# Causal attention: the mask of the scores by query moves from a TensorE matmul into VectorE's row maximum, and the maxima are split after their transpose

## The reference

```python
h = _layernorm(x, axis=-1) * (1 + ca) + sa
qkv = jnp.einsum('btc,fc->btf', h, W_attn)          # 16 heads of 32 channels
att = jnp.einsum('bhqd,bhkd->bhqk', q, k)
att = jnp.where(causal, att, -jnp.inf)
att = jax.nn.softmax(att / jnp.sqrt(32.), axis=-1)
out = jnp.einsum('bhqk,bhkd->bhqd', att, v)         # then W_proj
x = x + ga * attention
x = x + gb * mlp(modulated layernorm of x)          # three layers: 512-1024-1024-512
```

## Time and profile before

| | |
|---|---|
| median of 3 runs | 1666.01 us (1664.12 to 1668.75) |
| the profiled execution | 1668.86 us |
| its span | 1667.1 us |
| mean granted TensorE clock | 0.972 |
| PE busy | 1536.4 us, 92% of the span |
| DVE busy | 1000.6 us, 60% |
| ACT busy | 644.2 us, 39% |
| POOL busy | 370.6 us, 22% |

### The profile page before, as it was taken

One profiled execution on the slowest core, in us unless ns is written; L12 is line 12 of the kernel. 1 busy time (PEld: TensorE's weight loads), 2 busy tenths in 40 slices (PEclk: granted clock), 3 DMA queues, 4 the chain that ended last, 5 costly groups with the idle time before them and its releaser, 6 DMA issues.

```text
span 1667.1 us, 33396 instructions
## 1 busy us (share of the span) xinstructions
PE 1536.4 (92%) x12032; PEld 1345.7 (81%) x12032; DVE 1000.6 (60%) x2287; ACT 644.2 (39%) x1346; POOL 370.6 (22%) x360
## 2 busy tenths in 40 slices
PE   5499989898989898985699999999999999999998
PEld 1377777787777777874699999999999999999998
DVE  2477878878788878773844444445444454444442
ACT  2146666666666666674512122121212122121211
POOL 0224555454555554553000000000000000000000
PEclk9699999999999999996799999999999999999999
DMA  5162534243425252423600111001100011011100
GB/s 227 43 162 62 127 73 123 71 120 76 121 69 134 58 135 62 110 71 112 204 26 20 45 45 45 13 31 44 44 30 27 31 44 44 0 51 37 44 14 13
DMA packets 75272, 116.98 MB, mean 70 GB/s; under 512 B 10568, under 2 KB 27976, under 8 KB 74704
## 3 DMA queue, kind: packets, MB, share of 16 engines
q1 hardware_dynamic: 68816, 107.31, 23.4%
q10 hardware_dynamic: 6400, 8.92, 1.5%
HBM read 48.52 MB, written 16.81 MB: 39 GB/s over the span
## 4 chain that ended last, share of the span: by engine, by line
PE 51%; DVE 1%; DMA 1%; SPq 0%; ACT 0%; issue 0%; POOL 0%; DVEq 0%; POOLq 0%
PE feature L1203 33%; PE token L1184 16%; PE feature L1174 1%; PE token L1165 1%; DVE w L1115 1%; DMA b_rows<-b 0%; DMA w_ring<-wproj_t 0%; DVE y L1069 0%; SPq L945 0%; DVE y L1067 0%; ACT w L1021 0%; DVE attn_tiles L1093 0%; POOL mlp_rstd L982 0%; DVE gated L1077 0%; DVE res_tiles L1080 0%
## 5 line engine op out<-in xcount | busy, mean ns | idle before, releaser
L454 POOL TENSOR_TENSOR prob_lo<-prob,prob_hi 128x512 f16<-128x512 f32 x256 | 302.0, 1183 | 362.0 <-ACT prob L536 361.0
L1203 PE MATMUL feature<-y,w 128*128 128x256 f32 x3072 | 377.5, 284 | 5.1 <-DVE w L1115 5.1
L1203 PEld LDWEIGHTS feature<-y,w 128*128 128x128 f32 x3072 | 374.2, 190 | 6.7 <-DVE w L1115 5.3
L1015 ACT ACTIVATE mlp_full<-feature,b_cols 128x256 f32<-128x256 f32 x256 | 120.4, 476 | 647.0 <-PE feature L1203 617.4
L1067 DVE CAST y<-mlp_full 128x256 fp32r<-128x256 f32 x256 | 75.2, 294 | 302.4 <-ACT mlp_full L1015 302.1
L529 ACT ACTIVATE prob_hi<-key_score 128x512 f16<-128x512 f32 x320 | 192.3, 601 | 143.0 <-PE key_score L770 140.9
L708 PE MATMUL lin<-h_parts,wqkv 128*128 128x512 f32 x768 | 215.1, 403 | 9.5 <-DVE h_parts L585 9.5
L1203 PEld LDWEIGHTS feature<-turned,w 128*128 128x128 f32 x1536 | 189.2, 191 | 5.1 <-DVE w L1115 3.8
L1203 PE MATMUL feature<-turned,w 128*128 128x256 f32 x1536 | 189.7, 284 | 3.4 <-DVE turned L1069 3.4
L536 ACT ACTIVATE prob<-key_score 128x512 f32<-128x512 f32 x320 | 192.4, 601 | 0.0
L982 POOL TENSOR_TENSOR mlp_rstd<-mlp_var_eps,mlp_minus_half 128x2 f32<-128x2 f32 x16 | 11.1, 696 | 799.3 <-DVE mlp_var_eps L1088 799.3
(11 more groups left out here) (95 smaller groups left out, 1902.8 us busy)
## 6 DMA issues: line engine op xcount, KB each, us to landing
stack<-qk_parts SPq DMA_DIRECT2D x384, 128.0 KB, 2.4
x_tiles<-x SPq DMA_DIRECT2D x32, 256.0 KB, 3.1
attn_dram<-o_rows SPq DMA_DIRECT2D x32, 256.0 KB, 2.2
attn_tiles<-attn_dram SPq DMA_DIRECT2D x16, 512.0 KB, 4.4
res_tiles<-x SPq DMA_DIRECT2D x16, 512.0 KB, 3.6
out<-res_tiles ACTq DMA_DIRECT2D x16, 512.0 KB, 2.8
wmod_sb<-wmod SPq DMA_DIRECT2D x4, 1536.0 KB, 16.4
w_ring<-w_t SPq DMA_DIRECT2D x12, 512.0 KB, 6.2
```

Source lines behind the costliest of these rows:

```text
L454: nc.gpsimd.tensor_tensor(prob_lo[:, key[1] % 2, u, :], prob[:, u, :], prob_hi[:, key[1] % 2, u, :], ALU.subtract).then_inc(lo_pool, 1)
L1015: nc.scalar.activation(full[:, f % 2, :], fbank[f % 4][:, 0:CH], ACT.Relu, bias=bias[:, f:f + 1])\
L1203: mm = nc.tensor.matmul(fbank[f % 4][:, 0:CH], weights[:, wl, c, f * P:(f + 1) * P], data[:, dl, c, :], start=(c == 0 and i == 0), stop=(c ...
```

## The change

TensorE no longer writes the mask of the scores by query: only the mask by key is left (`mask_by_key`), and the first score matmul of a step starts its bank. `row_mask` is a tile of 128 x 512 in bf16, zero but for the triangle in its last 128 columns. VectorE adds its last n columns to a score tile of n columns, writes the sum back into the bank and takes the row maximum of it in the same instruction (`tensor_tensor_reduce`, line 672 of the changed kernel). Step 4, which took both of its tiles in one reduction, now has one instruction for each.

The maxima go on in another way: TensorE transposes the 8 columns of maxima as they are, ScalarE takes minus the transposed rows at step 1 into rows 0 to 7 of `max_rows`, VectorE makes the rest from the same PSUM bank at step 2 into rows 32 to 39, and SyncE, no longer ScalarE, issues the two DMAs, at step 2 of its own list. `max_rows` has one buffer where it had two, so ScalarE first waits until the DMAs of the pair before have landed.

Three more moves: ScalarE writes h twice from PSUM, once as float32 and once rounded, so that VectorE's rounding copy (line 583) goes, and TensorE's bank of a TURN item is free once ScalarE has read it; the lowest part of the values is made on GpSimd (`v_lowest`), no longer on VectorE; and the waits on `v_split` are counted anew (`v_before`).

```diff
-                nc.gpsimd.memset(mask_qk[:], 0.0).then_inc(pool_step, 1)
+                nc.gpsimd.memset(row_mask[:], 0.0).then_inc(pool_step, 1)
...
+                    turned = behind(b, p, 1, first)
+                    if u == 2 and turned:
+                        n, q = turned
+                        wait_apart(sp, turn_taken, 1 + PAIRS * n + q + 1, (o_out[0], 16))
+                        for part in range(2):
+                            sp.dma_start(f32(stack[3 * D + part:3 * D + part + 1, 0, 2 * q:2 * q + 2, :]),
+                                         f32(max_rows[LOW_ROWS * part:LOW_ROWS * part + 2 * NT, :]))\
+                                .then_inc(max_in[q], 16)
...
+                pool.wait_ge(v_mid_ready, v_no(n, g, t) + 1)
+                nc.gpsimd.tensor_tensor(v[:, t, hs, 0:D], rest, v[:, t, hs, 2 * D:3 * D], ALU.subtract)\
+                    .then_inc(v_split, 1)
...
-                nc.scalar.activation(full[:, c % 2, :], lin_bank_of((TURN, c))[:], ACT.Identity,
-                                     scale=mod_now[:, NC_ + c:NC_ + c + 1], bias=mod_now[:, c:c + 1])\
-                    .then_inc(lin_act, 1)
+                if c >= 2:
+                    act.wait_ge(lin_taken, LIN_CREDITS + lin_no(n, (TURN, c - 2)) + 1)
+                for made in (full[:, c % 2, :], h[:, 0, c, :]):
+                    last = nc.scalar.activation(made, lin_bank_of((TURN, c))[:], ACT.Identity,
+                                                scale=mod_now[:, NC_ + c:NC_ + c + 1], bias=mod_now[:, c:c + 1])
+                last.then_inc(lin_act, 1)
...
-                        nc.scalar.copy(max_rows[:, q % 2, :], turn_bank[0:4 * NT, 0:P]).then_inc(turn_taken, 1)
-                        act.wait_ge(turn_taken, 1 + PAIRS * n + q + 1)
-                        for part in range(2):
-                            act.dma_start(
-                                f32(stack[3 * D + part:3 * D + part + 1, 0, 2 * q:2 * q + 2, :]),
-                                f32(max_rows[2 * NT * part:2 * NT * (part + 1), q % 2, :]))\
-                                .then_inc(max_in[q], 16)
+                        act.wait_ge(max_in[(q - 1) % PAIRS], 32 * (n + 1 if q else n))
+                        nc.scalar.activation(max_rows[0:2 * NT, :], turn_bank[0:2 * NT, 0:P], ACT.Copy, scale=-1.0)\
+                            .then_inc(max_hi, 1)
...
-                        if u == 4:
-                            last = nc.vector.reduce_max(row_max[:, p % 2, :, 1],
-                                                        bank[:].rearrange("p (h k) -> p h k", h=2), AX.X)
-                        else:
-                            for _, hh, t, col in (r for r in BY_QUERY if r[0] == u):
-                                last = nc.vector.reduce_max(row_max[:, p % 2, hh, t:t + 1],
-                                                            bank[:, col:col + P * (t + 1)], AX.X)
+                        dve.sem_inc(score_seen, 1)
+                        for _, hh, t, col in (r for r in BY_QUERY if r[0] == u):
+                            n = P * (t + 1)
+                            last = nc.vector.tensor_tensor_reduce(
+                                out=bank[:, col:col + n], in0=bank[:, col:col + n], in1=row_mask[:, T - n:T], scale=1.0,
+                                scalar=LOWEST, op0=ALU.add, op1=ALU.max, accum_out=row_max[:, p % 2, hh, t:t + 1])
...
+                    turned = behind(b, p, 1, first)
+                    if u == 2 and turned:
+
+                        n, q = turned
+                        dve.wait_ge(max_hi, PAIRS * n + q + 1)
                         nc.vector.scalar_tensor_tensor(
-                            out=neg_max[:, p % 2, 1, :].bitcast(F32R), in0=peak, scalar=-1.0,
-                            in1=neg_max[:, p % 2, 0, :], op0=ALU.mult, op1=ALU.subtract).then_inc(max_ready, 1)
+                            out=max_rows[LOW_ROWS:LOW_ROWS + 2 * NT, :], in0=turn_bank[0:2 * NT, 0:P], scalar=-1.0,
+                            in1=f32(max_rows[0:2 * NT, :]), op0=ALU.mult, op1=ALU.subtract).then_inc(turn_taken, 1)
...
-                    nc.tensor.matmul(diagonals(bank, u, False), ident_bf[:], mask_for(mask_qk, u),
-                                     start=True, stop=False, skip_group_check=True)
```

More of the change, by code:

```diff
@@ L42 @@
 MASKED = -1e30
+LOWEST = -3.0e38
+LOW_ROWS = 32
 EPS = 1e-5
@@ L228, with diagonals @@
 LO_ON_DVE = (2,)
-def diagonals(bank, u, by_key):
-    first = {t: col if by_key else col + P * t for u2, _, t, col in (BY_KEY if by_key else BY_QUERY) if u2 == u}
+def diagonals(bank, u):
+    first = {t: col for u2, _, t, col in BY_KEY if u2 == u}
     if u in (0, 2):
@@ L311, in attention @@
     row_max = mem.sb("row_max", [P, 2, 2, NT])
-    neg_max = mem.sb("neg_max", [P, 2, 2, 2 * NT])
-    max_rows = mem.sb("max_rows", [4 * NT, 2, P], F32R)
+    max_rows = mem.sb("max_rows", [LOW_ROWS + 2 * NT, P], F32R)
     prob = mem.sb("prob", [P, UNITS, 512])
@@ L350, in v_no, with v_before @@
         return V_UNITS * n + NT * g + t
+    def v_before(g, t):
+        place = ORDER.index((V, g, t))
+        return max([NT * o[1] + o[2] + 1 for i, o in enumerate(ORDER[:place]) if o[0] == V and (place - i) % 2 == 0],
+                   default=0)
     def unit_no(b, p, u):
@@ L447, in _, with v_lowest @@
             pool.wait_ge(ones_ready, 2)
+            def v_lowest(n, item):
+                if item[0] != V or not last_item(item):
+                    return
+                g, t = item[1:3]
+                hs = slice(g * H // 2, (g + 1) * H // 2)
+                rest = full[:, ORDER.index((V, g, t)) % 2, 0:C // 2].rearrange("p (h d) -> p h d", d=D)
+                pool.wait_ge(v_mid_ready, v_no(n, g, t) + 1)
+                nc.gpsimd.tensor_tensor(v[:, t, hs, 0:D], rest, v[:, t, hs, 2 * D:3 * D], ALU.subtract)\
+                    .then_inc(v_split, 1)
+            for item in before_first():
+                v_lowest(0, item)
             def slot(b, p, first, more):
@@ L468, in slot @@
                             .then_inc(o_scaled, 1)
+                    for n, item in work(b, p, u, more):
+                        v_lowest(n, item)
                     if p == 2 and u == 4 and more:
@@ L619, in after_item @@
                     v_rest(n, item[1], item[2])
-            def step_after_item(n, item):
-                if item[0] == V and last_item(item):
-                    v_lowest(n, item[1], item[2])
             row_stats(0, range(NT))
@@ L722, in do_item @@
                 if item[0] == TURN or item[-1] == 0:
-                    pe.wait_ge(lin_taken, lin_no(n, unit_of(item)) + 1)
+                    place = ORDER.index(unit_of(item))
+                    if ORDER[place - 2][0] == TURN:
+                        pe.wait_ge(lin_act, lin_no(n, unit_of(item)) - 1)
+                    else:
+                        pe.wait_ge(lin_taken, lin_no(n, unit_of(item)) + 1)
                 if item[0] == TURN:
@@ L797, in slot @@
                     key = behind(b, p, 2, first)
-                    masks(b, p, u, key)
+                    if key:
+                        mask_by_key(*key, u)
                     if p < PAIRS:
```

76 lines of the change are left out of this document (28 added, 48 removed).

## The result

The changed kernel takes 1724.42 us (median of 4 runs, 1721.98 to 1728.28), the kernel before, run beside it, 1667.38 (1664.12 to 1670.23): 1.0345 times as long, interval 1.0316 to 1.0374. Forecast were 1716 us and 1684 to 1762.

The account below looks back on a forecast made before the run. PE was taken to bound attention, busy 78.14 of 85 us. From 1668.9 us, +37 for slots, +2 for the last batch and +11 for the clock made 1719; the median lies 2.9 lower, so 1716 us, range 1684 to 1762.

Parts of the forecast that it names:

- The path from step 2 to the landing: From step 2's scores by key to the maxima's DMAs landing: 5.6 us, where PE needs 5.02 in that slot.
- Slot by slot: Attention's slots: slots 0 to 2 and 4 shorter, 3 and 5 to 7 longer; +5.3 us a batch, +37 over seven.
- the half clock that was counted apart: Behind the stall ahead of slot 0: 3.2 us at half speed, 1.6 us lost each time.
- the 48 forecast: Seven batches of attention: +37 us from the slots and +11 from the clock.
- The clock: PE's clock halves once behind each of seven stalls ahead of slot 0: +11 us, 0 if it held.
- the long stall: Ahead of slot 0, PE waits for the maxima's DMAs behind SyncE's 12 stack DMAs and output: +5.1 us.
- The end of attention: The last batch's short slots, 7.3 to 8.2 us, get a floor of some 8.2: +2 us.
- The masks: Five mask matmuls fewer a slot on PE: 0.4 us a slot, 26 us in all if PE stays the bound.
- What was taken to cost nothing: VectorE's removed and added instructions about cancel, staying near 69 us a batch; GpSimd takes 64 subtractions into idle time.
- the rival with two cycles an element: Masked maximum on VectorE takes 2.7 us more a slot, VectorE becomes the bound: 1754 us, up to 1790; 10%.
- The 2.0 us of slot 4: Slot 4 shortens from 13.88 to 11.9 us as PE's banks come free earlier: -2.0 us.
- The rival of absorbed stalls: The maxima's DMAs land in time everywhere, so the masks and slot 4 gain in full: 1626 us; 6%.

Follow-up runs that it names:

- experiment 10: Kernel before with the masked maxima alone, VectorE's eight batches written out instead of a loop: 1659.4 us.
- experiment 12: Changed kernel with the old path of the maxima, VectorE's batches written out instead of a loop: 1645.4 us.
- experiment 11: As experiment 5, with VectorE's batches written out instead of a loop: 1637.3 us.
- experiment 7: Kernel before with the masked maxima alone, no mask matmul by query, max_rows with one buffer: 1681.7 us.
- experiment 8: Changed kernel with the old path of the maxima (neg_max on VectorE at slot's end, copy and DMAs on ScalarE at step 1): 1674.0 us.
- experiment 1: Changed kernel, but SyncE issues its blocks of 12 stack DMAs only behind the maxima's DMAs of the next step 2: 1698.6 us.
- experiment 3: Changed kernel with the edits of experiment 1 and experiment 2 together: 1668.9 us.
- experiment 9: Kernel before with 88 increments of an unused semaphore in VectorE's loop, nothing else: 1672.5 us.
- experiment 2: Changed kernel, but VectorE makes the rest of the maxima ahead of prob_lo in step 2: 1708.9 us.
- experiment 4: Changed kernel, but ScalarE issues the maxima's DMAs at the end of its step 2, VectorE's rest left in place: 1748.7 us.
- experiment 5: As experiment 3, with SyncE's loads of x also behind the maxima's DMAs of slot 0: 1639.9 us.
- experiment 6: As experiment 4, but VectorE makes the rest of the maxima ahead of prob_lo: 1684.9 us.

## Why the prediction was right, step by step

**The path from step 2 to the landing**: 5.6 us forecast, 5.10 measured. Its parts: the rest's instruction 0.28 (0.35 taken), from the issue's start to the landing 2.5 (0.62 + 2.4 = 3.0 taken, half a us too much, and so nearly the whole difference). That it equals the 5.02 of the earlier trace rows is why the plain slots kept their 9.4 us and gained nothing; 9.7 was forecast (its terms add up to 9.8).

**Slot by slot**: forecast 9.7 and measured 9.42 for slot 5, 13.2 and 12.87 for slot 3, 11.9 and 11.78 for slot 4, 11.9 and 11.68 for slot 6, 14.6 and 15.49 for slot 7, 30.1 and 31.70 for slots 0 to 2, which hold the half clock that was counted apart with 1.6. The sum is 93.0 and 92.94 for this batch; the sum over seven is 52.6 us instead of the 48 forecast, since the first two batches lose more. Slot 7's excess over 14.6 is in its front: VectorE's split of q and k, with which SyncE's block starts, comes 3.2 us into the slot (445.70; in the earlier trace rows 2.4 us). There PE runs at the clock of 0.50 from 443.5 on. In the one batch without that fall the split comes 2.5 us into the slot, in the six with it 2.8 to 3.9.

**The clock**: the fall behind the long stall came, seven times of seven, but the forecast counted one fall of 3.2 us a batch, and there are two, the other in slot 7. From 100 us on to the last batch the mean granted clock is 0.95 over 636 us, where it was 0.99 over 584. My estimate from these two rounded means is 26 us more of full clock lost, against 11 forecast. That slot 0 still came out at the forecast 11.3 us (mean of the seven; 10.9 to 12.1) and the sum at 93.0 is in part luck. The step from the earlier trace rows to one fall behind each stall was bolder than it looked: the same two waits of 1.2 and 1.3 us stand in slot 4 of every batch of the kernel before, and only two of the seven show a fall there. In the profiled executions the mean is 0.956 for 0.972.

**The end of attention** was sized too low: from slot 0 of the last batch on, the changed kernel needs 7.6 us more (736.93 to 814.58, against 684.32 to 754.33), where +2 was forecast. The four short slots behind slot 3 had been 6.5 to 8.0 us, not 7.3 to 8.2, and became 8.0 to 8.9: 4.8 us. Slot 0 behind the last stall and slot 3 add 1.6 and 1.8. With the 52.6 us of the seven batches this makes the 60 us.

**The masks**: 0.4 us a slot forecast, 0.47 measured (9.41 to 8.94) in slots that PE bounds, but 26 us in all was too much: alone they bring 10. Slots 3 and 2 gain 0.15 each, and slot 4, where PE waits for VectorE, loses 0.3 to 1.8 (experiment 10). It had little part in the result: slots 1 and 2 kept 0.3 and 0.2 us of the gain, slot 5, which ends with the landing, none.

**What was taken to cost nothing**: the masked maximum runs at 690 ns for 512 columns (674 for the plain one), so the rival with two cycles an element is out. The Trainium skill (Vector Engine (DVE) Microarchitecture Reference, points that are easy to get wrong) names the halving for an instruction shape with two sources, when both are in SBUF and not bf16; here one is in PSUM and the other bf16, and the trace shows no halving. Whether the masked maximum has that shape, no run shows. The read of the accumulator has 133 ns in its row (0.1 taken), but the next maximum starts at the same time as it. VectorE was forecast near 69 us a batch, as before; in the batch from 365.01 us it is busy 65.7, and over the span 965 us instead of 1001. The 2.0 us of slot 4 came in the changed kernel (11.78 for 13.88), with the new path. Without it they are less: experiment 12 against 10, the other moves alone, is 14.0 us, but not as 7 times 2.0. In their profiled executions slot 4 is 1.8 us shorter in the mean, and 5.8 us lie ahead of the first batch's first score by key (98.1 for 103.9 us).

**The rival of absorbed stalls** (1626 us) gave the right direction for mended kernels: 1637 when nearly all transfers are in time (14.9 us of waits on `max_rows` are left in experiment 11). What is left is mostly the masks' smaller worth (10 for 26 us); that split is argued, not shown.

**Missed altogether** was VectorE's idle at the return of its loop, 3 to 4 us, five times. Here a longer stall of PE lay beside it; in experiments 7 and 8 it cost 22 and 29 us (against experiments 10 and 12). That the forecast came out without it is luck.

## What to carry to other kernels

Where a DMA is moved to another engine's list, its cost is what stands ahead of it there: 12 issues of 0.64 us cost more than all that the change saved, and deferring them helps only until the next urgent DMA (experiments 1 and 3). Measure the parts of a change one by one: here a part worth 10 us looked like a loss of 13 because of a loop's return. And when a stall is taken away, look at once for idle time of other engines that it covered.

## What was not expected of the hardware

- VectorE stands idle for 2.9 to 4.0 us at each return of its loop in every kernel with masked maxima in the loop, 45 returns of 45 in the nine of them; in the kernel before and in experiment 9 it doesn't, and with the batches written out it doesn't. The rows of the loop's own line show where the time goes. Between the branch and the first instruction behind it, which only sets registers, are some 3.1 us in the changed kernel (first two rows) and 0.3 in experiment 9 (last two):

```profile
L384 DVEq COMPARE_BRANCH  x1: 63/63/63, 453.8 to 453.8; - x1
L384 DVEq FUSED_REGOPS  x1: 63/63/63, 456.9 to 456.9; - x1
...
L378 DVEq COMPARE_BRANCH  x1: 67/67/67, 342.9 to 342.9; - x1
L378 DVEq MOVE  x1: 36/36/36, 343.3 to 343.3; - x1
```

- So neither the masked maximum nor a wait for PE holds VectorE there; the time lies in front of both. The DMA queue that carries instructions says the same. From 256 to 680 us it has no packet in the kernel before or in experiment 9, and 23 in the changed kernel:

```profile
q14 instruction: 23, 0.19, 0.2%
```

- In experiment 7 two of them lie in the idle of 4.04 us at 432.4, in experiment 8 one in the second idle, in front of the read. The reading that fits all of this is that these kernels fetch VectorE's loop anew in each round, and that the two without idle do not. Experiment 10, written out, has 11 such packets in the same stretch and no idle: fetching straight on costs it nothing, the branch does. The Trainium skill (Runtime: NRT & Kernel Launch, instruction fetch mechanics) says that most engines hold two blocks of 256 instructions, and that a taken branch to outside of them has to fetch the target first; the trace agrees in kind. The bodies have 266 instructions (before), 354 (experiment 9), 352 (the change and experiments 1 to 6), 360 and 378 (8 and 7). All are under 512, so by that rule it would hang on where a body lies against the blocks as well, and 352 with an idle beside 354 without one shows that length alone does not decide. What does stays open. Shifting the body by some instructions ahead of the loop would tell; it was not tried.
- The two DMAs of the maxima, 4 KB each, had landed 2.5 us after the first one's issue began in a plain slot (428.26 to 430.78), and 3.0 us behind SyncE's block of 12 and an output (454.94 to 457.95).
